# First layer of a two-layer kernel: row maxima from two 64-row matmuls side by side in place of two 128-row ones

## What is computed

```python
h = group_norm(x, gn_w, gn_b)                      # 32 groups, (8, 512, 1024)
q, k, v = heads(qkv_w @ h + qkv_b)                 # 8 heads of 64 channels
attn = softmax(q.T @ k * 64 ** -0.5, axis=-1)      # 1024 x 1024 a head
x1 = x + proj_w @ (attn @ v.T) + proj_b
```

## Time and profile before

| | us |
|---|---|
| median of 3 runs | 2716.44 |
| the runs | 2716.44, 2714.8, 2719.52 |
| span of the profiled execution | 2718.4 |
| TensorE busy | 2619.7 (96%) |
| weight loads busy | 2181.7 (80%) |
| VectorE busy | 2055.1 (76%) |
| ScalarE busy | 1578.5 (58%) |
| GpSimd busy | 221.9 (8%) |

### The profile page before, as it was taken

One profiled execution on the slowest core, in us unless ns is written; L12 is line 12 of the kernel. 1 busy time (PEld: TensorE's weight loads), 2 busy tenths in 40 slices (PEclk: granted clock), 3 DMA queues, 4 the chain that ended last, 5 costly groups with the idle time before them and its releaser, 6 DMA issues.

```text
span 2718.4 us, 33180 instructions
## 1 busy us (share of the span) xinstructions
PE 2619.7 (96%) x11856; PEld 2181.7 (80%) x11856; DVE 2055.1 (76%) x3294; ACT 1578.5 (58%) x1930; POOL 221.9 (8%) x134
## 2 busy tenths in 40 slices
PE   6999999999999999999999999999999987899998
PEld 5788888888888888888888888888888876688887
DVE  6788768876887688768876887688767867878864
ACT  4667646764676467646764676567646663334311
POOL 1000000000000000000000000000000012111010
PEclk9999999999999999999999999999999999899999
DMA  4512232223222322232223222321322335466444
GB/s 156 177 50 80 67 103 61 79 71 100 64 78 67 101 67 76 63 107 67 65 72 109 66 59 79 109 67 48 90 83 58 112 127 203 171 215 246 165 164 170
DMA packets 154849, 279.48 MB, mean 103 GB/s; under 512 B 51776, under 2 KB 52032, under 8 KB 154176
## 3 DMA queue, kind: packets, MB, share of 16 engines
q1 hardware_dynamic: 152128, 268.98, 31.4%
q0 software_dynamic: 2560, 8.39, 1.0%
HBM read 180.04 MB, written 63.18 MB: 89 GB/s over the span
## 4 chain that ended last, share of the span: by engine, by line
PE 83%; DVE 9%; issue 3%; DMA 2%; ACT 1%; SPq 0%; POOL 0%; POOLq 0%; DVEq 0%; ACTq 0%
PE tiles L372 9%; PE tiles L373 8%; PE tiles L374 8%; PE tiles L474 8%; PE tiles L451 8%; PE tiles L428 8%; PE tiles L468 8%; PE tiles L467 8%; PE tiles L447 7%; PE tiles L1321 5%; PE tiles L1371 2%; DVE row_max L679 2%; DVE p_low L695 2%; DVE h_low L787 1%; PE tiles L383 1%
## 5 line engine op out<-in xcount | busy, mean ns | idle before, releaser
L679 DVE TENSOR_REDUCE row_max<-tiles 128x1 f32<-128x512 f32 x1014 | 694.5, 685 | 443.4 <-PE tiles L428 440.6
L544 ACT ACTIVATE p_high<-tiles 128x1024 fp32r<-128x1024 f32 x512 | 525.5, 1026 | 595.8 <-PE tiles L451 595.1
L695 DVE TENSOR_TENSOR p_low<-tiles,p_high 128x1024 fp32r<-128x1024 f32 x512 | 623.0, 1217 | 7.0 <-ACT tiles L546 6.2
L546 ACT ACTIVATE tiles<-tiles 128x1024 f32<-128x1024 f32 x512 | 523.0, 1021 | 0.0
L467 PE MATMUL tiles<-p_high,v_high 128*128 128x512 f32 x1024 | 406.5, 397 | 2.2 <-ACT num_den L562 1.5
L428 PE MATMUL tiles<-k_high_low,q_high_high 128*128 128x512 f32 x1014 | 404.8, 399 | 0.2 <-DVE row_max L679 0.2
L468 PE MATMUL tiles<-p_high,v_low 128*128 128x512 f32 x1024 | 402.0, 393 | 0.0
L428 PEld LDWEIGHTS tiles<-k_high_low,q_high_high 128*128 128x128 f32 x1014 | 312.5, 308 | 48.6 <-DVE row_max L679 5.7
L474 PE MATMUL tiles<-p_low,v_high 128*128 128x512 f32 x1024 | 325.8, 400 | 14.9 <-DVE p_low L695 14.6
L451 PE MATMUL tiles<-q_low_max,k_high_one 65*128 65x512 f32 x1024 | 325.8, 399 | 1.9 <-DMA q_low_max<-row_max_top 1.8
L372 PE MATMUL tiles<-h_high,w_high 128*128 128x512 f32 x768 | 304.6, 397 | 17.3 <-DVE row_max L679 8.3
(11 more groups left out here) (167 smaller groups left out, 3138.1 us busy)
## 6 DMA issues: line engine op xcount, KB each, us to landing
x_tiles<-in_x SPq DMA_DIRECT2D x64, 512.0 KB, 5.4
w_high<-w_split SPq DMA_DIRECT2D x126, 256.0 KB, 2.8
w_low<-w_split SPq DMA_DIRECT2D x126, 256.0 KB, 3.0
k_high_one<-k_high_low SPq DMA_DIRECT2D x128, 128.0 KB, 2.3
q_high_high<-q_high_high SPq DMA_DIRECT2D x128, 128.0 KB, 2.3
o_normed<-rec_rows SPq DMA_DIRECT2D x64, 256.0 KB, 3.7
x<-x_tiles SPq DMA_DIRECT2D x32, 512.0 KB, 4.0
x_full<-x SPq DMA_DIRECT2D x32, 512.0 KB, 8.3
```

The source lines that it names most:

```text
L544: nc.scalar.activation(ph[:, r, :], ring[:, r, :], ACT.Exp, scale=ATT_SCALE).then_inc(s_ph, 1)
L546: nc.scalar.activation(ring[:, r, :], ring[:, r, :], ACT.Exp, scale=ATT_SCALE).then_inc(s_p32, 1)
L679: nc.vector.reduce_max(mcol[:, h % 2, n, i:i + 1], max_bank(h, i, n)[:, :], AX_X).then_inc(s_mx, 1)
L695: tt(pl[:, r, :], ring[:, r, :], ph[:, r, :].bitcast(F32), ALU.subtract).then_inc(s_pl, 1)
```

## The change

- The two matmuls of a maximum block have 64 rows each and come one directly behind the other: high part of q times high part of k, the first 512 keys from partitions 0 to 63 and the second 512 keys from partitions 64 to 127. For the latter the second 512 keys of k's high part are copied to a new tensor `k_high_second` by DMA, two copies for each second k unit (64 in all). The low part of k is no longer in the row maximum. One semaphore increment for the pair.
- One VectorE reduce over 1024 columns replaces two over 512 and `top_of_halves` with its tensor.
- The pair stands behind the units of the step, ahead of `weigh_high`, or, in the 31 steps where two units are under way at once, ahead of the units (`pair_first`).
- For the pair to be read in one pass its banks lie side by side: the second half always takes the middle one of the three, the first half and the units one of the outer two. `pv` moves to another half of its bank pair.
- VectorE's order in a step is: low parts of the last step's units, the reduce, `p_low(t)` of the same step (before: of the step before).
- The first five blocks keep matmuls of 128 rows, with one reduce each.

```diff
-READ_BEHIND = dict(m=8, k=26, q=26, v=12, vt=28, o=26, g=22)
+READ_BEHIND = dict(m=9, k=26, q=26, v=12, vt=28, o=26, g=22)
+MIDDLE = 1
+def pair_first(h, s):
+    spans = (before(h, s), (h, s))
+    begun = {u for at in spans for u, parts in PARTS.get(at, []) if u[0] not in ("g", "vt")}
+    here = {u for u, _ in PARTS.get((h, s), [])}
+    going = {u for u in begun if u in here}
+    return len(going | here) > 1
...
-            at += 7
-            if block:
-                take(("m", *block, 0), before(h, s))
+            at += 6
+            if block and pair_first(h, s):
+                at += 1
+                for n in range(2):
+                    take(("m", *block, n))
             for u, parts in PARTS.get((h, s), []):
                 at += {"g": 1, "vt": 2}.get(u[0], 6 * len(parts))
                 take(u)
-            at += 5
-            if block:
-                take(("m", *block, 1))
+            if block and not pair_first(h, s):
+                at += 1
+                for n in range(2):
+                    take(("m", *block, n), UNITS.get((h, s), []))
+            at += 4
...
-    for e, closed in events:
-        open_banks = [i for i in range(BANKS) if closed is None or holder[i] not in UNITS.get(closed, [])]
+    for e, closed, at in events:
+        among = (MIDDLE,) if e[0] == "m" and e[-1] == 1 else (0, 2)
+        open_banks = [i for i in among if holder[i] not in closed and (holder[i] is None or end[holder[i]] <= at)]
...
-    sb("spare", [P, 2, N])
+    k3 = sb("k_high_second", [P, 4, HALF], F32R)
...
-    ring, pv = tiles[:, 0:2, :], tiles[:, 2, HALF:N]
-    banks = [tiles[:, 2, 0:HALF], tiles[:, 3, 0:HALF], tiles[:, 3, HALF:N]]
+    ring, pv = tiles[:, 0:2, :], tiles[:, 2, 0:HALF]
+    pool_row = tiles[:, 2:4, :].rearrange("p a n -> p (a n)")[:, HALF:(1 + BANKS) * HALF]
+    banks = [pool_row[:, i * HALF:(i + 1) * HALF] for i in range(BANKS)]
...
-        def take_max(h, i, n):
+        def take_max(h, i):
             g = h // 2
             if h % 2 == 0 and i == 0:
-                pe.wait_ge(s_kql, kq(("k", g, n)))
+                pe.wait_ge(s_kqh, kq(("k", g, 1)))
+                pe.wait_ge(s_second, 32 * (g + 1))
...
-            fill_free(("m", h, i, n))
+            for n in range(2):
+                fill_free(("m", h, i, n))
             first = (i // 4) * HALF + i % 4
-            mm(max_bank(h, i, n)[:, :], q1[:, q_slot(h), first:first + HALF - 3:4], k1[:, k_slot(h), n * HALF:(n + 1) * HALF],
+            to = max_banks(h, i)
+            mm(banks[to[0]], q1[0:HD, q_slot(h), first:first + HALF - 3:4], k1[0:HD, k_slot(h), 0:HALF],
+               start=True, stop=True)
+            mm(banks[to[1]], q1[HD:P, q_slot(h), first:first + HALF - 3:4], k3[HD:P, k_slot(h), :],
                start=True, stop=True).then_inc(s_max, 1)
...
             scores(h, s)
-            if block:
-                take_max(*block, 0)
+            if block and pair_first(h, s):
+                take_max(*block)
             for u, parts in PARTS.get((h, s), []):
                 unit_work(u, parts)
+            if block and not pair_first(h, s):
+                take_max(*block)
             if t > 0:
                 weigh_high(t - 1)
-            if block:
-                take_max(*block, 1)
...
+        def reduce_max(h, i):
+            if h > 1 and i % 4 == 0:
+                dve.wait_ge(s_mrow[i // 4], 16 * (h - 1))
+            dve.wait_ge(s_max, h * NT + i + 1)
+            first = min(max_banks(h, i))
+            nc.vector.reduce_max(mtop[:, h % 2, i:i + 1], pool_row[:, first * HALF:(first + 2) * HALF], AX_X
+                                 ).then_inc(s_mx, 1)
...
             if t > 0:
-                behind = before(h, s)
-                done = max_tile(*behind)
-                if done:
-                    reduce_max(*done, 1)
-                    if done[1] % 4 == 3:
-                        top_of_halves(done[0], done[1] // 4)
-                p_low(t - 1)
+                for u in UNITS.get(before(h, s), []):
+                    unit_low(u)
             if block:
-                reduce_max(*block, 0)
-            if t > 0:
-                for u in UNITS.get(behind, []):
-                    unit_low(u)
+                reduce_max(*block)
+            p_low(t)
...
                 sp.dma_start(to[:, w, cols].bitcast(F32), high[:, w, cols].bitcast(F32)).then_inc(s_twin[kind, i], 16)
+                if kind == "k" and i == 1:
+                    sp.dma_start(k3[HD:P, w, :].bitcast(F32), k1[0:HD, w, cols].bitcast(F32)).then_inc(s_second, 16)
...
-            sp.wait_ge(s_mtop, 2 * h + i + 1)
+            sp.wait_ge(s_mx, h * NT + 4 * i + 4)
```

More of the change, by code:

```diff
@@ L141, with take @@
 BANKS = 3
-READ_BEHIND = dict(m=8, k=26, q=26, v=12, vt=28, o=26, g=22)
+READ_BEHIND = dict(m=9, k=26, q=26, v=12, vt=28, o=26, g=22)
[6 more added lines that the diff above has]
+    return len(going | here) > 1
 def bank_events():
     events, at, last = [], 0, {}
-    def take(e, closed=None):
+    def take(e, closed=()):
         if e not in last:
-            events.append((e, closed))
+            events.append((e, closed, at))
         last[e] = at
@@ L242, in attention_layer @@
     v32 = sb("v_full", [P, HALF])
-    mcol = sb("row_max", [P, 2, 2, NT])
+    sb("spare", [P, 2, 2, NT])
     mtop = sb("row_max_top", [P, 2, NT], F32R)
@@ L306, in fill_of, with max_banks @@
         return banks[BANK[u]]
-    def max_bank(h, i, n):
-        return banks[BANK["m", h, i, n]]
+    def max_banks(h, i):
+        return [BANK["m", h, i, n] for n in range(2)]
     h32 = Count([(0, 0)] + [(b, t) for b in range(1, BATCH) for t in range(CT)])
@@ L328, in tensor, with max_count @@
         mm = nc.tensor.matmul
-        def max_count(h, i, n):
-            return (h * NT + i) * 2 + n + 1
+        def max_count(h, i):
+            return h * NT + i + 1
         def fill_free(u):
@@ L337, in fill_free @@
             if w[0] == "m":
-                pe.wait_ge(s_mx, max_count(*w[1:]))
+                pe.wait_ge(s_mx, max_count(*w[1:3]))
             elif w[0] == "g":
@@ L403, in unit_work, with take_first_max @@
                 project(u, parts)
-        def take_first_max(i, n):
-            if n == 0 and i % 4 == 0:
+        def take_first_max(i):
+            if i % 4 == 0:
                 pe.wait_ge(s_kqh, kq(("q", 0, i // 4)))
@@ L410, in take_first_max @@
                 pe.wait_ge(s_kql, kq(("k", 0, 1)))
-            m = i * 2 + n
-            if m > 3:
-                pe.wait_ge(s_mx, m - 3)
+            if i > 1:
+                pe.wait_ge(s_mx, i - 1)
             first = (i // 4) * HALF + i % 4
-            mm(ring[:, i % 2, n * HALF:(n + 1) * HALF], q1[:, 0, first:first + HALF - 3:4],
-               k1[:, 0, n * HALF:(n + 1) * HALF], start=True, stop=True).then_inc(s_max, 1)
-        def take_max(h, i, n):
+            for n in range(2):
+                last = mm(ring[:, i % 2, n * HALF:(n + 1) * HALF], q1[:, 0, first:first + HALF - 3:4],
+                          k1[:, 0, n * HALF:(n + 1) * HALF], start=True, stop=True)
+            last.then_inc(s_max, 1)
+        def take_max(h, i):
             g = h // 2
             if h % 2 == 0 and i == 0:
-                pe.wait_ge(s_kql, kq(("k", g, n)))
+                pe.wait_ge(s_kqh, kq(("k", g, 1)))
+                pe.wait_ge(s_second, 32 * (g + 1))
             if h % 2 == 0 and i % 4 == 0:
@@ L435, in scores @@
             else:
-                pe.wait_ge(s_mx, 2 * (NT - AHEAD))
+                pe.wait_ge(s_mx, NT - AHEAD)
             if h % 2 == 0 and s % 4 == 0:
@@ L497, in tensor @@
                 for i in range(4):
-                    for n in range(2):
-                        take_first_max(i, n)
+                    take_first_max(i)
             if u == ("v", 0, 1):
-                for n in range(2):
-                    take_first_max(4, n)
+                take_first_max(4)
         pe.wait_ge(s_pset, 3)
@@ L665, in split_low, with reduce_first_max @@
             tt(low, raw, high.bitcast(F32), ALU.subtract).then_inc(s_rawl, 1)
[L667 to L670, removed]
+        def reduce_first_max(i):
+            dve.wait_ge(s_max, i + 1)
+            nc.vector.reduce_max(mtop[:, 0, i:i + 1], ring[:, i % 2, :], AX_X).then_inc(s_mx, 1)
         def normed_first(t):
@@ L852, in vector @@
         for i in range(4):
[L853 to L857, removed]
+            reduce_first_max(i)
+        reduce_first_max(4)
         for u in PROLOGUE[6:]:
@@ L1255, in free @@
                     elif SLOT1[u] == 2:
-                        pe.wait_ge(told["s_mx"], 2 * NT * ALL_HEADS)
+                        pe.wait_ge(told["s_mx"], NT * ALL_HEADS)
                         pe.wait_ge(told["s_nd"], 2 * ALL_HEADS)
                     else:
+                        pe.wait_ge(told["s_mx"], NT * ALL_HEADS)
                         pe.wait_ge(told["s_kql"], told["units_read"][0])
```

14 lines of the change are left out of this document (1 added, 13 removed).

## The result

The changed kernel takes 2896.01 us (2892.37 to 2896.67, 4 runs), the one before 2717.98 us beside it (2714.8 to 2721.58, 4 runs): ratio 1.0646, 95% interval 1.0631 to 1.0661, so 178 us slower. The forecast was 2774, the range 2640 to 2880. The mean granted clock is 0.992 in the profile of either kernel, so the clock is not part of the difference.

What follows compares the result with a forecast made beforehand. TensorE, busy 96% at 0.23 us a matmul, was taken as the bound. Array -15, bank waits +78 and eased low-part waits -5 gave +58 us on the 2716.4 median: 2774 us, range 2640 to 2880.

Steps and rivals of the forecast that it cites:

- bank term: Row maxima waiting for k and q units' banks: 0.75 us lost 68 times, 1.90 lost 14 times, +78 us.
- array term: Each pair's matmuls and loads on TensorE: 0.02 to 0.04 us less than before, 507 times, -15 us.
- The bound and the pitch: TensorE bounds the kernel, busy 96% of the span; a 512-column matmul costs 0.23 us, whatever its rows.
- serial loads: On TensorE a pair's two strided weight loads run one after the other, second half 0.2 us later; -15 us.
- Rival A: On TensorE both halves and their loads run together: -117 us for the array, 2672 us in all; chance 0.32.
- rival B: TensorE's array empties before and after each pair, 0.33 us a pair: 2837 us, or 2938 with serial loads; chance 0.24.
- the reduce: On VectorE one pass over 1024 columns takes 1.22 us, replacing two of 685 ns, all beside TensorE.
- credit of 5 us: Less work on VectorE eases TensorE's waits for low parts: 5 us credited of their 40.
- The start: At the kernel's start five reduces of 1.22 us replace ten of 0.68: under 1 us.
- The copies on SP: 64 more copies of k on SP's queue, their issue covered and TensorE's wait for them met: no cost.

Runs made afterwards that it cites:

- e2: Changed kernel with the pair's 128 queries read side by side instead of every fourth: 2841.57 us, ratio 1.0439.
- e5: Changed kernel with both 64-row matmuls of a pair on the same row half, partitions 0 to 63: 3020.31 us, ratio 1.1085.
- e6: Kernel before the change, with only the first matmul of each block at 64 rows, the second at 128: 2938.38 us, ratio 1.0795.
- e3: Changed kernel with each pair issued twice, one right behind the other into the same banks: 3009.26 us, ratio 1.1056.
- e9: Changed kernel with each 64-row pair issued three times in a row: 3130.05 us, ratio 1.1509.
- e10: Kernel of e1 (128 rows) with each pair issued three times in a row: 3269.87 us, ratio 1.2028.
- e1: Changed kernel, with its order, banks and single reduce, but both matmuls of a pair at 128 rows: 2822.87 us, ratio 1.0366.
- e7: Kernel of e1 with VectorE's order in each step reduce, then this step's units, then the low part: 2775.12 us, ratio 1.0191.
- e8: Kernel of e7 without the second copies of k and TensorE's wait for them: 2774.55 us, ratio 1.019.

## Why the prediction was wrong

**The direction was right, the size not**: +58 forecast, +178 measured, and the range ended 16 us short. The sign came from the bank term (+78); the array term had the wrong sign.

**The bound and the pitch** were right. 0.23 us a matmul carries the numbers above.

**The array term is the step that failed**: "I take the serial loads, -15 us". It assumed two things that the trace after denies. The loads of the halves do not follow each other, they run together. And a load is not fetched under a matmul of another row split: it begins with its own matmul, behind the gap, so it lies bare. In place of -15 us the pitch gives +142. Runs show the bare strided load (e2), the running together (e5), the price of one matmul alone (e6) and that it is paid by the visit (e3, e9, e10); how the rest divides into emptying and the bare load behind is read from the timeline alone. By the prediction's own signs this is B with A's loads: the second half at once, and 0.87 us from the matmul before the pair to the one behind.

**Rival A** was right about the halves (e5), rival B about the emptying, and neither about the loads. With the loads together B gave 0.10 us a pair over before. It had 0.33 for emptying, by the recorded length of a matmul; that is 0.09 + 0.10, so 0.14 too much. It had nothing for bare loads, 0.21 + 0.11. 0.10 - 0.14 + 0.32 = 0.28, which is measured. The numbers for both loads stood in the earlier trace rows, behind a wait, where nothing covered them; the step from "a wait bares a load" to "a change of split bares it too" was not made. The Trainium skill ("TensorEngine Tiling (Array Packing)", "Tiling Modes") says that changing the tiling mode drains TensorE; the trace agrees as far as it goes, with gaps of 0.09 and 0.10 us. The Trainium skill also says in "TensorE: Matmul & The Clock Gate", Part 3, that matmuls on different row groups start some 4 ns apart; the trace agrees, 3 or 4 ns.

**The bank term** was right: 82 places, 78 us; with the array at its old pace (e1) 82 places, 80.0 us, in the changed kernel 83 and 64.3. It did not add to the array's term, though. Each of the 83 waits contains the 0.35 us that the loader would stand anyway, so only 64.3 - 83 x 0.35 = 35 us count on top (39 by the starts, all waits of the visits included). That 142 + 35 = 177 comes so near the measured 178 is partly luck, since smaller terms cancel. Between the first row maximum and the last the stretch is 168 us longer: 145 for the visits at their median (1.213 us, against 0.927 in e1), 39 for waits there, 22 less for low parts, and 6 for all else. The other 8 us lie ahead of it and behind it. The prediction softened its +78 to +70 for B, which was far too little.

**VectorE**: the reduce was right, 1.22 us, all of it beside TensorE. The credit of 5 us was too small: the loads' waits for low parts fell from 25.2 to 3.8 us, and by the starts the stream waits 22 us less for them, in the changed kernel and in e1. Whether that is the shorter work or VectorE's new order no run separates; with the order of e7 the gain is 15. What hides it in e1 is on the other side: 80.0 us of waits for units' banks, and units that wait for a row maximum's bank, which the prediction did not look at (19.2 us before transposes of v). The start, put at under 1 us, is 2 to 3 us longer: the first score matmul is at 49.4 us, was 46.5.

**The copies on SP** at nothing: right (e8).

## What to carry to other kernels

A matmul on a row half of TensorE saves time only in company: going from 128-row matmuls to 64-row ones and back costs 0.51 us here, whatever is done in between, so in a full stream more than two pairs must stand in one visit (from 1.7 here, where waits cover part of the price), the first of them and the first matmul behind with the shortest load. When an operation leaves the engine's usual mode, cost what was hidden because of that mode (here the weight loads), not only the operation. Two waits at the same place do not add: the longer one covers most of the other.

## What the runs showed of the hardware

- The two row halves load and compute at the same time: both loads at 1001.47, both matmuls at 1001.47 (the second matmul 3 or 4 ns later in each of the 507 pairs).
- No weight load is fetched across a change of the row split. The first matmul on either side of it begins with its load, 0.21 us strided by 16 bytes, 0.11 plain (e2: 0.11 us less between pair and next load).
- A gap of 0.09 to 0.10 us, called emptying here, stands at each change. A matmul of 65 rows is no change: in the changed kernel's timeline L470, twice L474 and L389 follow at 1003.51, 1003.97 and 1004.44, two places in each 0.46 to 0.47 us.
- A single 64-row matmul pays the same as a pair (e6: 0.54 us to the next load).
